# Four-layer graph kernel: a deeper ring of edge records in the build, another split of signs and lower halves in the first attention layer, other places for the dense layers

## What is computed

```python
x = x + agg(h * out_deg**-0.5) * in_deg**-0.5            # layer 0: plain sum over edges
# layers 1, 2 (one GAT of two) and 3 (one GAT): for each edge and each added self loop
alpha = leaky_relu(s_src[src] + s_dst[dst], 0.2)
w     = exp(alpha - max_per_dst(alpha)); out = sum_dst(w * h[src]) / (sum_dst(w) + 1e-16)
# last layer: twice  relu(sum_dst(cat[x_dst, x_src, edge_weight] @ W + b)), then log_softmax
```

## Time and profile before

| | before |
|---|---|
| time, median of 3 runs | 2899.02 us (2898.58 to 2900.27) |
| time of the profiled execution | 2893.96 us |
| its span, first to last instruction | 2892.1 us |
| mean granted TensorE clock | 0.944 of full speed |
| PE busy | 2474.3 us, 86% |
| DVE busy | 2132.6 us, 74% |
| ACT busy | 1592.4 us, 55% |
| POOL busy | 377.0 us, 13% |

### The profile page before, as it was taken

How to read it: one execution, slowest core, us unless ns; L and a number is a source line. 1 busy time by engine, 2 the same in 40 slices (tenths; PEclk the granted TensorE clock), 3 DMA queues, 4 the chain that set the end, 5 groups by cost and what they waited for, 6 DMA issues and landing times. The chain is left out here.

```text
span 2892.1 us, 85900 instructions
## 1 busy us (share of the span) xinstructions
PE 2474.3 (86%) x31025; PEld 2221.1 (77%) x31026; DVE 2132.6 (74%) x4880; ACT 1592.4 (55%) x1992; POOL 377.0 (13%) x921
## 2 busy tenths in 40 slices
PE   3757998999899679999699998769999967999998
PEld 2645676676677569999599988659999867888997
DVE  8987888888798856767698988889999985221212
ACT  6014444444444279999788888488888840000101
POOL 1003445454444300000000000000000000000000
PEclk8878999999999889999899999889999988999999
DMA  3003443433433446767255565324555526888998
GB/s 105 0 0 85 124 125 92 129 114 104 124 106 113 131 157 217 252 223 242 92 197 184 187 215 177 133 68 159 198 197 181 178 100 239 309 311 293 321 358 299
DMA packets 398051, 494.35 MB, mean 171 GB/s; under 512 B 81925, under 2 KB 397289, under 8 KB 397674
## 3 DMA queue, kind: packets, MB, share of 16 engines
q1 hardware_dynamic: 275832, 408.76, 41.9%
q10 hardware_dynamic: 121972, 82.31, 9.3%
HBM read 401.81 MB, written 89.17 MB: 170 GB/s over the span
## 5 line engine op out<-in xcount | busy, mean ns | idle before, releaser
L2674 PE MATMUL psum<-sb_arena 128*128 128x198 bf16 (+2 forms) x14406 | 1097.6, 238 | 127.3 <-DVE sb_arena L1964 61.4
L2674 PEld LDWEIGHTS psum<-sb_arena 128*128 128x128 f16 x14406 | 1056.9, 99 | 157.8 <-DVE sb_arena L1964 73.4
L3289 ACT ACTIVATE sb_arena<-sb_arena 128x896 f16 (+1 forms) x1029 | 1009.7, 1060 | 141.7 <-PE psum L2674 84.3
L1954 DVE TENSOR_TENSOR sb_arena<-sb_arena 128x896 f16<-128x896 f16 x1029 | 630.7, 623 | 158.5 <-ACT sb_arena L3289 136.3
L2954 ACT ACTIVATE sb_arena<-psum 128x784 f16<-128x784 f32 x392 | 323.1, 824 | 414.7 <-PE psum L2319 227.8
L1242 DVE TENSOR_SCALAR sb_arena<-sb_arena 128x392 f16<-128x392 f16 x1960 | 476.3, 317 | 0.0
L2319 PE MATMUL psum<-sb_arena 64*128 64x392 f16 x3920 | 400.3, 343 | 78.2 <-ACT sb_arena L2954 35.6
L2746 PE MATMUL psum<-sb_arena 128*128 128x192 bf16 x4802 | 413.7, 247 | 27.2 <-DVEq L2089 15.7
L2746 PEld LDWEIGHTS psum<-sb_arena 128*128 128x128 f16 x4802 | 402.9, 98 | 36.8 <-DVEq L2089 16.4
L2319 PEld LDWEIGHTS psum<-sb_arena 64*128 64x128 bf16 x3920 | 259.1, 138 | 170.9 <-issue 109.3
L1964 DVE TENSOR_TENSOR sb_arena<-sb_arena 128x896 f16<-128x896 f16 x588 | 363.9, 619 | 3.3 <-PE psum L2688 1.7
(11 more groups left out here) (378 smaller groups left out, 1270.1 us busy)
## 6 DMA issues: line engine op xcount, KB each, us to landing
sb_arena<-counts SPq DMA_DIRECT2D x245, 896.0 KB, 6.8
sb_arena<-counts SPq DMA_DIRECT2D x245, 672.0 KB, 4.6
counts<-sb_arena ACTq DMA_DIRECT2D x56, 1344.0 KB
sb_arena<-records SPq DMA_DIRECT2D x392, 5.0 KB, 2.2
sb_arena<-records ACTq DMA_DIRECT2D x392, 5.0 KB, 2.3
counts<-sb_arena SPq DMA_DIRECT2D x1, 5488.0 KB
records<-sb_arena SPq DMA_DIRECT2D x1, 3124.0 KB, 8.9
counts<-sb_arena ACTq DMA_DIRECT2D x14, 112.0 KB
```

Of the source, the lines that this page charges most:

```text
L1954: nc.vector.tensor_tensor(above_at[r % RING], above_at[r % RING], counts_of(g, j), ALU.mult).then_inc(above_ready, 1)
L2674: last = nc.tensor.matmul(psum[:, bank, at:at + wide], of[:, b * BLK:(b + 1) * BLK], moves[side][:, r, :], start=(r == 0 and at == 0), sto ...
L3289: nc.scalar.activation(above_at[r % RING], of, ACT.Sigmoid, bias=steep_s[:, r:r + 1], scale=STEEP).then_inc(signs_ready, 1)
```

## The change

There are three parts.

1. Build: the ring `rec` gets RS = 14 slots, and one semaphore serves two neighbouring slots, so a wait is for the records of both. POOL may be 8 windows ahead (AHEAD, and WS = 8, which is now only the credit between POOL and DVE). ACT issues the first 14 loads ahead of its loop.
2. First attention layer (l = 0): of each seven tiles DVE makes the mask of tile 3 itself and multiplies in the same instruction (`scalar_tensor_tensor` with `is_gt` and `mult`, from the fp32 scores of the destinations); ACT leaves these out. For tiles 1 and 5 of each seven DVE subtracts the product from the counts, so that side 1 takes the true lower part, and PE's side 0 needs only the 99 columns of `up`. Layers 1 and 2 keep their work; their semaphore counts move.
3. Last layer: in each `first_pass` PE does `first_dense` after group 4 and `second_dense` after the seventh group. All six passes are now in the loop, and the call behind the loop is gone.

```diff
-WS = 7
+WS = 8
+RS = 14
+OWN_SIGN = 3
+WITH_BELOW = (1, 5)
...
-        rec_in = [sem("rec_in%d" % s) for s in range(WS)]
+        rec_in = [sem("rec_in%d" % s) for s in range(RS // 2)]
...
+        def own_sign(l, r):
+
+            return l == 0 and r % GRP == OWN_SIGN
+
+        def with_below(l, r):
+
+            return not whole(l, r) if l > 0 else r % GRP in WITH_BELOW
...
-                pool.sem_inc(rel_ready, WS)
+                pool.sem_inc(rel_ready, RS)
...
-                    s, w = k % WS, h * WH + k
-                    pool.wait_ge(rec_in[s], h * 128 + 32 * (k // WS + 1))
+                    s, w = k % RS, h * WH + k
+                    pool.wait_ge(rec_in[s // 2], h * 128 + 64 * (k // RS + 1))
...
-                AHEAD = 6
+                AHEAD = 8
...
+                    if own_sign(l, r):
+                        of = ROW2[:, bass.ds(c * CW, CW)] if not isinstance(c, int) else ROW2[:, c * CW:(c + 1) * CW]
+                        if not (isinstance(c, int) and c == 0 and r < RING):
+                            dve.wait_ge(tile_used, c * NB + (n * ROWS + r + 1 - RING))
+                        nc.vector.scalar_tensor_tensor(above_at[r % RING], of, against[:, r:r + 1], counts_of(g, j), ALU.is_gt, ALU.mult).then_inc(above_ready, 1)
...
-                        if l > 0 and r > 0:
+                        if r > 0 and (l > 0 or with_below(l, r - 1)):
                             count_below(c, r - 1)
...
-                        wide = moves[side].shape[2]
+                        wide = wide3 if l == 0 and with_below(l, r) else moves[side].shape[2]
...
-            def first_pass(c, second):
+            def first_pass(c):
 
                 for g in range(NGRP):
-                    if g == 0 and second:
-                        second_dense(c - 2)
                     pass_group(c, g, 4, H, 0, CHUNKS)
                     if g == 3:
                         turn_sums(c - 1)
-                first_dense(c - 1)
+                    if g == 4:
+                        first_dense(c - 1)
+                second_dense(c - 1)
                 pe.wait_ge(agg_kept, c + (2 * CHUNKS + 1))
...
-            first_pass(1, False)
-            with pe.Fori(2, CHUNKS) as c:
-                first_pass(c, True)
-            second_dense(CHUNKS - 2)
+            with pe.Fori(1, CHUNKS) as c:
+                first_pass(c)
...
-                            if not isinstance(w, int) or w + WS < NWIN:
-                                act.wait_ge(rel_ready, w + (WS + 1))
-                                second_group(h, k + WS)
+                            if not isinstance(w, int) or w + RS < NWIN:
+                                act.wait_ge(rel_ready, w + (RS + 1))
+                                second_group(h, k + RS)
...
-                for k in range(WS):
+                for k in range(RS):
                     second_group(0, k)
...
-                        signs(c, r)
+                        if not own_sign(l, r):
+                            signs(c, r)
```

More of the change, by code:

```diff
@@ L174, in gnn_kernel @@
         sub_iota, o = view(build_at, [BLK, NB * SUB], fp16)
-        rec, o = view(o, [BLK, WS, ST * 4], fp32)
+        rec, o = view(o, [BLK, RS, ST * 4], fp32)
         rel, o = view(o, [BLK, WH, ST * 3], fp32)
@@ L429, in gnn_kernel @@
         steep_s, tail = view(tail, [BLK, NB], fp32)
+        against = under_s
         above, tail = view(tail, [BLK, NB], fp32)
@@ L484, in whole, with sign_tiles, signs_before @@
             return l == 1 and r % GRP in WHOLE
+        def own_sign(l, r):
+            return l == 0 and r % GRP == OWN_SIGN
+        def with_below(l, r):
+            return not whole(l, r) if l > 0 else r % GRP in WITH_BELOW
+        def sign_tiles(l, r=NB):
+            return sum(not own_sign(l, k) for k in range(r))
+        def signs_before(l):
+            return sum(CHUNKS * sign_tiles(k) for k in range(l))
         def below_tiles(l, r=NB):
-            return sum(not whole(l, k) for k in range(r))
+            return sum(with_below(l, k) for k in range(r))
         def below_before(l):
-            return CHUNKS * below_tiles(1) if l == 2 else 0
+            return sum(CHUNKS * below_tiles(k) for k in range(l))
         def groups_full(l):
@@ L1915, in split_attention @@
                         nc.vector.tensor_scalar(steep_s[:], scores[:, :, 0], STEEP, None, ALU.mult)
+                        if l == 0:
+                            nc.vector.tensor_scalar(against[:], scores[:, :, 0], -1.0, None, ALU.mult)
                         if l != 1:
@@ L2039, in chunk @@
                         count_above(c, r)
-                        if l > 0 and r > 0:
+                        if r > 0 and (l > 0 or with_below(l, r - 1)):
                             count_below(c, r - 1)
-                        elif l > 0 and not first:
+                        elif r == 0 and l > 0 and not first:
                             count_below(c - 1, NB - 1)
@@ L2673, in tile @@
                             seen.add(k)
-                            last = nc.tensor.matmul(psum[:, bank, at:at + wide], of[:, b * BLK:(b + 1) * BLK], moves[side][:, r, :],
+                            last = nc.tensor.matmul(psum[:, bank, at:at + wide], of[:, b * BLK:(b + 1) * BLK], moves[side][:, r, 0:wide],
                                                     start=(r == 0 and at == 0), stop=(r == NB - 1), skip_group_check=True)
-                            if l == 0 and side == 1 and b == 0:
+                            if l == 0 and side == 1 and b == (CB - 1 if with_below(l, r) else 0):
                                 last.then_inc(tile_used, 1)
```

15 lines of the change are left out of this document (8 added, 7 removed).

## The result

| | before | after |
|---|---|---|
| median of 11 runs each, same chip | 2899.4 us | 2891.04 us |
| profiled execution, its span | 2893.96, 2892.1 | 2889.32, 2886.4 |

What follows compares the result with a forecast made beforehand. PE, busy nine tenths, was taken to bound the build, ACT's signs the first attention layer, PE (97%) the last stage. Build +2, layer -27, stage +1 make -24: 2870 from 2893.96, or 2875 against the median; range 2858 to 2899.

Steps and rivals of the forecast that it cites:

- Build, the start: Build: ACT's seven more load issues at 1.36 each delay its first eviction, for which PE waits: +9.5 us.
- Build, what the ring gives back: Build: the deeper ring cuts PE's waits by 7.7 us (0 to 35.7), leaving the build at +2.
- Layer, what the engines have to do: First attention layer: work per chunk becomes ACT 41.1, PE 42.3, DVE 41.3 us, from 47.7, 46.0 and 30.5.
- the rival at 2.0: Rival 4, first attention layer: DVE's own sign takes 2.0 instead of 1.0, about 50 a chunk, 2914 us; chance 0.07.
- Layer, what balance costs: First attention layer: three nearly equal engines make a chunk of 43.5 us, little above the largest; layer -27.
- rival 1: First attention layer: three balanced engines stall each other as in the second layer, 45.9 a chunk, 2892 us; chance 0.17.
- The ends of this term: First attention layer: its gain is -36 us with 42.3 a chunk and -10 with 45.9.
- Last stage: Last stage: moved dense layers give -0.4 a pass, -2.4, and jumps +3: +1 us, ends -2.4 and +22.
- The bare jump: Last stage: PE's loop jump with an empty queue costs 0.5 a pass, +3; rival 3 has +22, chance 0.08.
- three signs of being wrong: Build shorter by more than 10 us, first-layer chunks above 45.5, or a bare jump adding over 1.5 per last-stage pass.

Runs made afterwards that it cites:

- `l0_light`: Kernel before with only the change's first-layer part, DVE's lower halves left out at tiles 8, 12 and 15: 2873.76 us, ratio 0.9891 to 0.9921.
- `last_only`: Kernel before with only the change's last-stage part (dense layers moved, six passes in one loop): 2895.55 us, ratio 0.9966 to 0.9986.
- `build_thirds4`: Kernel before with the change's build part, one of POOL's three sums of thirds done four times: 2918.93 us, ratio 1.0041 to 1.0068.
- `light_last_sp3`: Kernel before plus `l0_light`'s first layer, the change's last stage, and 3 of ACT's 28 record loads a half issued by SP: 2858.94 us.

## Why the prediction was right or wrong

- **Build, the start: right.** First eviction at about 243.5 forecast, 242.2 found; 8.2 of the 9.5.
- **Build, what the ring gives back: wrong in sign, and most of the miss.** The step was "I take the middle of the two rows that name DVE, 4.3 and 11.0, or 7.7", under the bound "At the least it is nothing". The halves gave back nothing and took 8.8 (6 to 11 in the other runs with loads 14 ahead). No row excluded a loss: the waits that the change was to remove say what it can give, not what the loads that come earlier cost on ACT, DVE and POOL. The runs show that the distance of the loads costs it (689.2 with 7 ahead, 699.4 with 14, nothing else changed). By which engine it reaches PE is open: the remedy was on ACT's side, and more load on DVE changed nothing. +17 instead of +2: 15 us.
- **Layer, what the engines have to do: right.** DVE's fused operation took 1.15 (forecast 1.08), and the next started 1.07 behind it; the rival at 2.0 is out. The Trainium skill (Vector Engine (DVE) Microarchitecture Reference, "Points that are easy to get wrong") says that this form "with two non-bf16 SBUF sources halves throughput". As the prediction read that, as 2.0 for 896 elements, this trace does not agree. The three engines ended between 90.6 and 92.4 of 100 in 45.28, so at 41 to 42, as summed.
- **Layer, what balance costs: wrong in size.** The step was "In the first layer the fold is short (4.0, which is less than five PE tiles, of a ring of seven), so I take **43.5**". A ring of seven covers a stretch only if it is full when the stretch begins. DVE was 91% busy and stood three to four tiles ahead of PE (PE worked on for 2.8 after the fold began), and the stretch was 5.2, not 4.0, since the change itself had put tile 12's lower half behind the fold. Of it PE saw 2.4 and ACT 2.4, in every chunk. That is rival 1, near its price (45.9 forecast, 45.28 found); `l0_light`, which relieves DVE around the fold only, came to 43.9, near where I had put the change. Inner chunks -12 instead of -21, the first -5 (forecast -4), the last 0 instead of -2: 9 us. The ends of this term do not follow from its parts either: 42.3 a chunk gives about -33 (5 x 5.4 + 6) and not -36, and 45.9 gives -15 and not -10.
- **Last stage: the mechanism right, two sizes off, and a gain that nothing forecast.** A pass gained 0.16, not 0.4: from the end of a pass (2469.34) to the next (2472.07) are 2.7, where I had 2.3 for DVE's sums. The bare jump cost nothing that a row shows, where I had 0.5. By these two the six passes gain 1.0. The rest of the trace's 5.7 came from stops and waits that were no part of the argument: two stops of 1.4 and one of 1.6 that the kernel before had, less the 1.6 by which the first pass began later, and 1.8 less waiting for transfers at the end. So +1 was -6 in the trace (-7 by `last_only`'s times). Such stops come and go between kernels whose last stage is the same, so this gain is not one to rely on.
- Sum: +15, +9, -7 on a forecast of -24 is -7, and -8.4 was measured. That the sign came out right and the time inside the range is partly luck: without the last stage's unforeseen 7 the change would have been within 2 us of the kernel before.
- None of the three signs of being wrong that the prediction names came up: the build did not get shorter, the chunks stayed (just) below 45.5, and no jump added 1.5 to a pass. It had no sign for a build that gets longer.

## What to carry over

A long wait in a profile need not say what its removal is worth; ask who waits for the waiter, and what the way of removing it adds elsewhere. Here taking away POOL's wait of 304 us by loading further ahead made the build longer, while three of ACT's loads, moved to another queue, were worth 7 us, with PE's waits for ACT only 31 before. When engines are balanced to within some per cent, a long piece of work on one of them that a ring used to hide comes out at half its length or more (2.4 of 4.0 here), and what the program has put behind it waits as well; lighten the tiles beside it, or cut it up, and leave one engine (here PE, at 96%) as the bound. Before deepening a prefetch, count what its prologue puts on the engine that must also do the first eviction.

## What the hardware showed

- Two engines' SBUF work does meet: a group of ten DVE key operations of 392 takes 2.4 alone or beside POOL's short operations, and 2.8 to 3.2 beside a POOL sum of 65 to 260 elements or a self loop of 128 x 128 (up to 4.0 where four such sums follow one another, `build_thirds4`). POOL's sum of 15 elements takes from 0.2 up to over 2 us beside DVE.
- The same code in the last stage took 271.9 to 279.7 us in the traces of kernels that differ only in the first layer, with stops of 1.4 to 1.6 inside runs of matmuls that no semaphore explains, and 276.7 in `light_last_sp3`, which differs from the first of them only in the build. A gain of under 5 us in a kernel of this size needs the stretch itself measured, not only the total.
